# A macaron transformer on one core: products of the second attention moved into its bursts, its norm steps moved to GpSimd

## The chip, the cores and the metric

The kernel runs on one core of one Trainium2 chip. The metric is the device time of one launch in microseconds. The core has TensorE (PE, matmuls and transposes, results to PSUM), VectorE (DVE), ScalarE (ACT), GpSimd (POOL) and SyncE (SP). Each engine takes its instructions in the order of its own queue, and engines are tied by semaphores only.

## The reference, cut to what matters

The input is 8 x 512 tokens of 128 numbers. Six blocks follow one another, each on the normalized x and each added to x:

```
x = x + 0.5 * ffn0(norm(x));  x = x + attn0(norm(x));  x = x + 0.5 * ffn0(norm(x))
x = x + 0.5 * ffn1(norm(x));  x = x + attn1(norm(x));  x = x + 0.5 * ffn1(norm(x))
```

The change is in attn1, the second attention. It has 16 heads of 8 numbers and compares every query of a sequence with every key by a hyperbolic distance:

```
diff_sq  = max(q_norm_sq + k_norm_sq - 2.0 * qk, 0.0)
denom    = max((1.0 - q_norm_sq) * (1.0 - k_norm_sq), 1e-06)
cosh_arg = max(1.0 + 2.0 * diff_sq / denom, 1.0)
attn     = softmax(-arccosh(cosh_arg)); out = (attn @ v) @ Wo.T
```

After it comes the layer norm of the new x (mean and variance over the 128 numbers), and router logits for the last block.

## The kernel before, in words

x stays in SBUF for the whole launch (X, tokens on partitions; XT, the normalized x turned round). The phases F0a, A0, F0b, F1a, A1, F1b follow one another, with a barrier between them. A1 (`attn1`, from line 1106) is the phase of the change. One iteration of its loop is one chunk: 512 tokens, one sequence. `main(0, True)` is the first chunk, without a predecessor; a loop runs `main(c, False)` for chunks 1 to 7, and code behind the loop finishes chunk 7.

For each head a 512x512 square of scores is made in two halves, so a chunk has 32 halves, numbered n. PE makes the squared distance (`difference(n)`, 28 rows of KT and QT, line 1592) and the factor 1/denom (`factor(n)`, 9 rows, line 1604). DVE takes the first with a clamp (`relu`, line 1455) into a U slot and multiplies the second in (`scale`, line 1463). ACT makes from a whole head two square roots (lines 1418 and 1419), POOL adds their results (`add`, line 1373), and ACT takes a logarithm and an exponential (lines 1428 and 1430), into a Y slot. PE multiplies Y with the values (`outputs`, line 1576), where the two heads of a pair use different columns; pair p is heads 2p and 2p + 1. There are four U slots (relu of head h waits for the add of head h - 4) and six Y slots (the first root of head h waits for the products of the pair that used the slot).

The order of the work is written by hand, engine by engine. DVE and PE go in four bursts a chunk, each for four heads, eight halves, steps i = 0 to 7. In step i PE issues `difference(n0 + i + 1)` (i from 1 to 6), `factor(n0 + i)` and then whatever `after(i)` holds; DVE does the next relu, the scale, and its own `after(i)`. The stretches between bursts are called gaps here:

- Burst 0 holds turns (transposes of the assembled q and k rows, line 1307, copied by DVE at line 1315) in steps 0 to 3. In the gap behind it the next chunk's q, k and values are projected (line 1200) and taken by DVE (`take_q_vector`, `take_k_vector`, `take_v_vector`, lines 1224 to 1252), with products of pairs 6 and 7 of the chunk before between the projections.
- Burst 1 holds the turning and dividing of the chunk before's output. In the gap behind it come the output projection, the addition to x (line 465), the norm's statistics (lines 115 to 120, ending in var_eps) and products of pairs 0 and 1.
- Burst 2 holds the norm: `norm_apply_vector` (line 126) in step 1, the turn of the normed rows in step 3, the router logits in step 5. POOL makes rstd (line 140) between the adds of heads 3 and 4.
- The gap behind burst 2 has four turns with products of pairs 2 and 3 between them, burst 3 four more turns, and the gap behind it four turns with products of pairs 4 and 5 of the chunk before (the calls stand at the top of the next `main`).

ACT works in groups of four heads: eight roots, a table load, four pairs of logarithm and exponential, a table load. At the start of A1 POOL copies the first rows of x, clears the row buffers QA and KA (lines 1359 and 1360, memory of the last phase's weights) and VA, and writes constant columns; DVE waits for all of it (`pad_ready`) before its first take. Of a row of 64 numbers in QA and KA the matmuls use numbers 0 to 27 and 32 to 40 only.

Of the kernel before, what the change touches and what calls it, by code (L numbers as in the profile page):

```python
# [5 lines left out]
ALU = mybir.AluOpType  # L6
# [7 lines left out]
P = 128  # L14
# [20 lines left out]
def macaron(nc, x, alpha, w_qkv0, bias_rows0, wo0, wo0_t, wfc0, router0, expert_bias, up0, down0,  # L35
            w_qkv1, wo1, router1, up1, down1, out, stop_after=99):
    ctx = ExitStack()
    with ctx:
# [1090 lines left out]
        def attn1():  # L1129
# [14 lines left out]
            with ExitStack() as st:  # L1144
# [172 lines left out]
                def early_bank(i):  # L1317
                    return (i + 2) % 6

                (turn_out_tensor, divide_vector, turn_back_tensor, _, project_out_tensor,  # L1320
                 residual_vector) = tail_steps(s, lay, lambda t, g: OT[:, g, t * P:(t + 1) * P], on, oT, rden[:, :], ROWS)
# [5 lines left out]
                def turn_norm_tensor(eng, n):  # L1327
                    eng.wait_ge(s["xn_ready"], n + 1)
                    eng.wait_ge(s["x_added"], n)
                    for t in range(TPC):  # L1330
                        last = eng.transpose(ps[:, ROWS, t * P:(t + 1) * P], xn[:, t, :], ident[:, :])
                    last.then_inc(s["tr_done"], 1)

# [21 lines left out]
                def body(block):  # L1355
                    @block.gpsimd
                    def _(eng):
                        eng.tensor_copy(xa[:, :], XT[:, 0:S]).then_inc(s["xa_ready"], 1)
                        eng.memset(QA.rearrange("p h r -> p (h r)").bitcast(F32), 0.0)
                        eng.memset(KA.rearrange("p h r -> p (h r)").bitcast(F32), 0.0)  # L1360
                        eng.memset(VA[:, :], 0.0)
                        eng.drain()
                        eng.memset(QA[:, :, 26:28].bitcast(F32), 1.0)
                        eng.memset(KA[:, :, 24:26].bitcast(F32), 1.0)
                        eng.memset(KA[:, :, 40:41].bitcast(F32), FAR)
                        eng.memset(VA[:, 0:TPC * H * VC].rearrange("p (h r) -> p h r", r=VC)[:, :, HD:HD + 1], 1.0)
# [9 lines left out]
                        def main(c, first):  # L1376
# [5 lines left out]
                            if not first:  # L1382
                                norm_gpsimd(eng, s, c)
# [15 lines left out]
                        norm_gpsimd(eng, s, B)  # L1399
# [39 lines left out]
                    def _(eng):  # L1439
# [6 lines left out]
                        def main(c, first):  # L1446
# [64 lines left out]
                            if tail:  # L1511
                                residual_vector(eng, c, before_c)
                                norm_stats_vector(eng, s, c, before_c)
# [21 lines left out]
                        eng.wait_ge(pad_ready, 1)  # L1535
# [13 lines left out]
                        residual_vector(eng, B, B - 1)  # L1549
                        norm_stats_vector(eng, s, B, B - 1)  # L1550
                        norm_apply_vector(eng, s, B, B - 1)
# [5 lines left out]
                    def _(eng):  # L1557
# [23 lines left out]
                        def main(c, first):  # L1581
# [68 lines left out]
                            if not first:  # L1650
                                outputs(c - 1, 6, (0, 1))
                            eng.wait_ge(s["q_taken"], c + 2)
                            project_rows_tensor(eng, xa, 1, ROWS, "k_done")
                            if not first:
                                outputs(c - 1, 6, (2, 3))
                                outputs(c - 1, 7, (0, 1, 2, 3))
# [4 lines left out]
                            def after1(i):  # L1661
                                if first:
# [48 lines left out]
                        project_rows_tensor(eng, xa, 1, 7, "k_done")  # L1711
                        eng.wait_ge(s["asm_done"], 1)
# [8 lines left out]
                        for pair in range(4, PAIRS):  # L1721
# [79 lines left out]
```

## Time and profile before

| | us |
|---|---|
| three runs, median (lowest, highest) | 3533.08 (3528.67, 3537.28) |
| the profiled execution: time | 3532.39 |
| the profiled execution: span | 3530.7 |
| busy: PE | 2876.4 |
| busy: DVE | 2279.0 |
| busy: ACT | 1908.5 |
| busy: POOL | 850.3 |
| mean granted clock of TensorE, share of full | 0.837 |
| phase A1, first and last activation of ACT in it | 1848.0 and 3065.2 (starts) |

Times in the rows are microseconds from the start of the span. Busy time of PE counts overlapping matmul records once, and a busy PE need not be at its peak. The granted clock is given as a share of 2.4 GHz: 0.50 is 1.2 GHz. In brackets behind a row stands how long the engine had been idle before it, and which instruction ended that.

### The profile page before, as it was taken

The page shows a single profiled execution, that of the slowest core. Times are in us where ns is not written, and L with a number is a line of the kernel's source. Part 1 is how long each engine was busy: PE and PEld are TensorE (multiplying, and loading weights), DVE is VectorE, ACT ScalarE, POOL GpSimd, SP SyncE. Part 2 cuts the span into 40 slices and gives each one's busy share as a digit, 9 for nine tenths or more (in the row PEclk, how much of TensorE's full clock was granted, in tenths as well). Part 3 has the DMA queues.
Part 4 walks back from the last instruction along what each step waited for, and adds up shares of the span by engine and source line. Part 5 has one row for each costly group of instructions (what it writes and reads, how often), then busy time and mean ns, then how long its engine had stood idle before and what let it go on. Part 6 is the DMA issues. An engine that isn't in the chain of part 4 may idle for free. (4 is left out here: it accounts for less than half of the span.)

```text
span 3530.7 us, 52885 instructions
## 1 busy us (share of the span) xinstructions
PE 2876.4 (81%) x17862; PEld 2183.2 (62%) x17862; DVE 2279.0 (65%) x5078; ACT 1908.5 (54%) x2244; POOL 850.3 (24%) x546
## 2 busy tenths in 40 slices
PE   5999968888599996999966767767676776679999
PEld 4888856666488885999952333333333333269998
DVE  5555557777555556666656776776676777366665
ACT  2222257676422222334318888887888888633333
POOL 1000010000000001000025555554655555410000
PEclk9999979999799997999975666666666666689999
DMA  2000000000000001000000000000000000010000
GB/s 78 0 0 0 0 1 1 0 0 0 0 1 0 0 0 48 0 0 0 0 0 0 1 1 0 0 0 0 0 0 0 0 0 0 0 48 0 0 0 24
DMA packets 3189, 17.98 MB, mean 5 GB/s; under 512 B 1088, under 2 KB 2112, under 8 KB 2112
## 3 DMA queue, kind: packets, MB, share of 16 engines
q1 hardware_dynamic: 3136, 17.32, 1.3%
q8 instruction: 28, 0.46, 0.1%
q14 instruction: 25, 0.20, 0.0%
HBM read 15.22 MB, written 2.10 MB: 5 GB/s over the span
## 5 line engine op out<-in xcount | busy, mean ns | idle before, releaser
L1373 POOL TENSOR_TENSOR A_Y<-A_Y,A_U 128x2048 f32<-128x2048 f32 x96 | 433.5, 4541 | 419.5 <-ACT A_U L1419 419.5
L1604 PE MATMUL ps<-A_QT,A_KT 9*128 9x512 f32 x512 | 294.3, 671 | 247.4 <-DVE A_U L1463 247.4
L1455 DVE TENSOR_SCALAR A_U<-ps 128x1024 f32<-128x1024 f32 x256 | 309.0, 1217 | 81.2 <-POOL A_Y L1373 50.4
L140 POOL TENSOR_TENSOR rstd<-var_eps,half_neg 128x4 f32<-128x4 f32 x45 | 49.8, 1107 | 1277.9 <-DVE var_eps L120 1277.9
L1604 PEld LDWEIGHTS ps<-A_QT,A_KT 9*128 9x128 f32 x512 | 120.0, 290 | 376.8 <-DVE A_U L1463 354.7
L1463 DVE SCALAR_TENSOR_TENSOR A_U<-ps,A_U 128x1024 f32<-128x1024 f32 x256 | 311.7, 1218 | 49.3 <-PE ps L1604 49.3
L1592 PE MATMUL ps<-A_QT,A_KT 28*128 28x512 f32 x512 | 269.7, 662 | 88.2 <-DVE A_U L1455 86.8
L257 ACT ACTIVATE F1b_act<-ps 128x512 f32<-128x512 f32 x256 | 153.3, 599 | 247.4 <-PE ps L223 231.4
L257 ACT ACTIVATE F1a_act<-ps 128x512 f32<-128x512 f32 x256 | 153.3, 599 | 242.9 <-PE ps L223 226.6
L257 ACT ACTIVATE F0b_act<-ps 128x512 f32<-128x512 f32 x160 | 95.7, 598 | 273.1 <-PE ps L223 273.1
L1419 ACT ACTIVATE A_U<-A_U 128x2048 f32<-128x2048 f32 x128 | 242.5, 1894 | 0.0
L231 PEld LDWEIGHTS ps<-dn,F1a_hT 128*128 128x128 f32 x2048 | 237.2, 192 | 4.4
L231 PEld LDWEIGHTS ps<-dn,F1b_hT 128*128 128x128 f32 x2048 | 237.2, 192 | 4.4
L257 ACT ACTIVATE F0a_act<-ps 128x512 f32<-128x512 f32 x160 | 95.7, 598 | 266.1 <-PE ps L223 266.1
L231 PE MATMUL ps<-dn,F1a_hT 128*128 128x128 f32 x2048 | 237.6, 275 | 0.0
L231 PE MATMUL ps<-dn,F1b_hT 128*128 128x128 f32 x2048 | 237.6, 275 | 0.0
L1418 ACT ACTIVATE A_Y<-A_U 128x2048 f32<-128x2048 f32 x96 | 182.5, 1901 | 80.7 <-DVE A_U L1463 51.4
L841 ACT ACTIVATE A_M<-A_M,A_nmax 128x192 f32<-128x192 f32 (+1 forms) x512 | 203.9, 471 | 35.4 <-DVE A_nmax L956 34.1
L1592 PEld LDWEIGHTS ps<-A_QT,A_KT 28*128 28x128 f32 x512 | 126.1, 294 | 133.2 <-DVE A_U L1455 107.2
L956 DVE CUSTOM_DVE_ANT_0 A_M<-ps,A_mask 128x192 f32<-128x192 f32 (+1 forms) x512 | 169.2, 387 | 48.0 <-PE ps L1007 47.2
L1576 PE MATMUL ps<-A_Y,A_VA 128*32 128x512 f32 x768 | 176.2, 672 | 17.1 <-ACT A_Y L1430 17.1
L1430 ACT ACTIVATE A_Y<-A_Y 128x2048 f32<-128x2048 f32 x96 | 183.4, 1911 | 6.5
(334 smaller groups left out, 6673.0 us busy)
## 6 DMA issues: line engine op xcount, KB each, us to landing
dn<-in_down SPq DMA_DIRECT2D x2, 2048.0 KB, 12.0
stage<-in_up SPq DMA_DIRECT2D x1, 2560.0 KB, 9.2
X<-in_x SPq DMA_DIRECT2D x1, 2048.0 KB, 7.8
F1a_up<-in_up SPq DMA_DIRECT2D x1, 2048.0 KB, 7.8
F1b_up<-in_up SPq DMA_DIRECT2D x1, 2048.0 KB, 7.3
out_x<-X SPq DMA_DIRECT2D x1, 2048.0 KB, 6.3
dn<-in_down SPq DMA_DIRECT2D x1, 1280.0 KB, 11.9
qkv_w_s<-in_w_qkv SPq DMA_DIRECT2D x2, 192.0 KB
```

The source lines that it names most:

```text
L231: last = eng.matmul(ps[:, 4 + d % 2, t * P:(t + 1) * P], hT[:, d % 2, hb, t * P:(t + 1) * P], dn[:, d, hb, :], start=(hb == 0), stop=(hb = ...
L257: eng.activation(act_out[:, j % RING, :], ps[:, (j * G) % 4, :], ACT.Silu if lay == 0 else ACT.Relu).then_inc(s["act_done"], 1)
L841: last = eng.activation(m, m, ACT.Exp, scale=-1.0, bias=nmax[:, n % MR, b, r:r + 1])
L1373: eng.tensor_tensor(flat(y_slot(h)), flat(y_slot(h)), flat(Um[:, h % UR]), ALU.add).then_inc(s["t_ready"], 1)
L1418: eng.activation(y, u, ACT.Sqrt, bias=1.0)
L1419: eng.activation(u, u, ACT.Sqrt).then_inc(s["s_ready"], 1)
L1430: eng.activation(y, y, ACT.Exp, scale=-1.0 if square_on_vector(h) else -2.0).then_inc(s["y_exp"], 1)
L1455: eng.tensor_scalar(u_half(h, half), d_pair(n), 0.0, None, ALU.max).then_inc(s["dp_vector"], 1)
L1463: eng.scalar_tensor_tensor(out=u, in0=g_pair(), scalar=CLAMP, in1=u, op0=ALU.min, op1=ALU.mult).then_inc(s["u_ready"], 1)
L1576: last = eng.matmul(ps[j:j + 32, OUT, :], VA[:, v0:v0 + 32], y_slot(h)[:, kt, :], start=(kt == 0), stop=(kt == TPC - 1))
L1592: last = eng.matmul(ps[:, 2 * (n % 2) + b, :], KT[r:r + 28, h // 2, kt * P:(kt + 1) * P], QT[r:r + 28, h // 2, :], start=True, stop=True)
L1604: last = eng.matmul(ps[:, 4 + b, :], KT[r:r + 9, h // 2, kt * P:(kt + 1) * P], QT[r:r + 9, h // 2, :], start=True, stop=True)
```

## The change

- The two halves of the products of pairs 0, 2, 4 and 6 (the first pair of each group of four heads) leave the gaps. They are issued behind `factor` in steps 5 and 6 of a burst: pair 6 of the chunk before in burst 0, pair 0 in burst 1, pair 2 in burst 2, pair 4 in burst 3. The products of pair 7 are spread over the two places where pair 6 was.
- The addition of the attention's output goes to xa (a buffer of q's input, free by then) and not into X (`add_back_vector`), and the statistics are taken from xa. POOL makes rstd, then subtracts and multiplies in four instructions, and copies xa into X (`apply_norm_gpsimd`). DVE no longer does these steps in burst 2.
- The clearings of QA and KA are left out, the constant columns are written first, and the wait for `pad_ready` moves from DVE to PE, behind the first projections.

```diff
+                def add_back_vector(eng, n, chunk):
+                    eng.wait_ge(s["o_done"], n)
+                    eng.tensor_tensor(xa[:, :].rearrange("p (t d) -> p t d", d=D), tiles_of(chunk),
+                                      ps[:, ROWS, :].rearrange("p (t d) -> p t d", d=D), ALU.add).then_inc(s["x_added"], 1)
+                    eng.drain()
+                    for t in range(TPC):
+                        eng.bn_stats(bn[:, t, :], xa[:, t * D:(t + 1) * D])
+                    eng.drain()
...
+                def apply_norm_gpsimd(eng, n, chunk):
+                    norm_gpsimd(eng, s, n)
+                    eng.drain()
+                    for t in range(TPC):
+                        eng.tensor_scalar(xn[:, t, :], xa[:, t * D:(t + 1) * D], mv[:, t, 0:1], rstd[:, t:t + 1],
+                                          ALU.subtract, ALU.mult)
+                    eng.drain().then_inc(s["xn_ready"], 1)
+                    eng.tensor_copy(tiles_of(chunk), xa[:, :].rearrange("p (t d) -> p t d", d=D))
+                    eng.drain()
...
-                        eng.memset(QA.rearrange("p h r -> p (h r)").bitcast(F32), 0.0)
-                        eng.memset(KA.rearrange("p h r -> p (h r)").bitcast(F32), 0.0)
-                        eng.memset(VA[:, :], 0.0)
-                        eng.drain()
                         eng.memset(QA[:, :, 26:28].bitcast(F32), 1.0)
                         eng.memset(KA[:, :, 24:26].bitcast(F32), 1.0)
                         eng.memset(KA[:, :, 40:41].bitcast(F32), FAR)
+                        eng.memset(VA[:, :], 0.0)
+                        eng.drain()
...
                             if not first:
-                                norm_gpsimd(eng, s, c)
+                                apply_norm_gpsimd(eng, c, last_chunk(c))
...
                             def after2(i):
-                                if tail and i == 1:
-                                    norm_apply_vector(eng, s, c, before_c)
...
-                        eng.wait_ge(pad_ready, 1)
                         take_q_vector(eng, 0, 6)
...
                             turn(c, EARLY)
-                            if not first:
-                                outputs(c - 1, 4, (0, 1))
                             turn(c, EARLY + 1)
-                            if not first:
-                                outputs(c - 1, 4, (2, 3))
...
                             def after0(i):
                                 if i < 4:
                                     turn(c, EARLY + 4 + i)
+                                if not first and i in (5, 6):
+                                    outputs(c - 1, 6, (2 * i - 10, 2 * i - 9))
...
                             def after1(i):
+                                if i in (5, 6):
+                                    outputs(c, 0, (2 * i - 10, 2 * i - 9))
...
-                            outputs(c, 0, (0, 1, 2, 3))
                             outputs(c, 1, (0, 1, 2, 3))
 
                             def after2(i):
+                                if i in (5, 6):
+                                    outputs(c, 2, (2 * i - 10, 2 * i - 9))
...
                             turn(c + 1, 0)
-                            outputs(c, 2, (0, 1))
                             turn(c + 1, 1)
-                            outputs(c, 2, (2, 3))
...
                             def after3(i):
                                 if i < 4:
                                     turn(c + 1, 4 + i)
+                                if i in (5, 6):
+                                    outputs(c, 4, (2 * i - 10, 2 * i - 9))
...
                         project_rows_tensor(eng, xa, 1, 7, "k_done")
+                        eng.wait_ge(pad_ready, 1)
                         eng.wait_ge(s["asm_done"], 1)
```

## Rows read from the trace of the kernel before

**Rows 1.** Windows, one chunk of A1: stretch, length, busy by engine, clock, DMA.

```profile
2006.27:2159.89 153.62, 109.28 (x386) 52.57 (x384) 109.08 (x122) 128.35 (x72) 83.58 (x45) 0.64 0.00 0
```

**Rows 2.** Timeline of ACT: start, length, instruction, idle time before it.

```profile
2006.27 1.28 ACT L1418 ACT_TABLE_LOAD   x1 [12.57 <-PE ps L1576]
...
2088.40 1.91 ACT L1418 ACTIVATE dn<-A_U 128x2048 f32<-128x2048 f32 x1 [8.80 <-PE ps L1576]
...
2123.70 1.91 ACT L1418 ACTIVATE A_Y<-A_U 128x2048 f32<-128x2048 f32 x1 [2.82 <-PE ps L1576]
...
2138.08 1.91 ACT L1430 ACTIVATE A_Y<-A_Y 128x2048 f32<-128x2048 f32 x1
...
2159.89 1.28 ACT L1418 ACT_TABLE_LOAD   x1 [12.34 <-PE ps L1576]
```

**Rows 3.** Timeline of DVE over the same chunk and the next burst 0.

```profile
2015.99 2.35 DVE L1455 TENSOR_SCALAR A_U<-ps 128x1024 f32<-128x1024 f32 x2 [6.19 <-POOL A_Y L1373]
...
2043.73 0.17 DVE L120 TENSOR_SCALAR var_eps<-mv 128x4 f32<-128x4 f32 x1
...
2049.68 2.36 DVE L1455 TENSOR_SCALAR A_U<-ps 128x1024 f32<-128x1024 f32 x2 [1.87 <-POOL dn L1373]
...
2056.44 7.25 DVE L126 TENSOR_SCALAR xn<-X,mv,rstd 128x128 f32 x4
...
2079.74 1.23 DVE L1463 SCALAR_TENSOR_TENSOR A_U<-ps,A_U 128x1024 f32<-128x1024 f32 x1 [1.31 <-PE ps L1604]
...
2093.78 2.35 DVE L1455 TENSOR_SCALAR A_U<-ps 128x1024 f32<-128x1024 f32 x2
...
2115.36 1.22 DVE L1463 SCALAR_TENSOR_TENSOR A_U<-ps,A_U 128x1024 f32<-128x1024 f32 x1 [1.31 <-PE ps L1604]
...
2129.08 2.34 DVE L1455 TENSOR_SCALAR A_U<-ps 128x1024 f32<-128x1024 f32 x2
...
2150.51 1.22 DVE L1463 SCALAR_TENSOR_TENSOR A_U<-ps,A_U 128x1024 f32<-128x1024 f32 x1 [1.31 <-PE ps L1604]
```

**Rows 4.** Timeline of PE: a projection, products at either clock, factors of burst 0.

```profile
1997.79 2.08 PE L1200 MATMUL ps<-qkv_w_s,A_xa 128*128 128x128 f32 x8
...
2081.60 3.63 PE L1576 MATMUL ps<-dn,A_VA 128*32 128x512 f32 x8
...
2088.79 1.91 PE L1576 MATMUL ps<-A_Y,A_VA 128*32 128x512 f32 x8
...
2144.19 0.79 PE L1604 MATMUL ps<-A_QT,A_KT 9*128 9x512 f32 x1 [1.57 <-DVE A_U L1463]
...
2149.25 0.79 PE L1604 MATMUL ps<-A_QT,A_KT 9*128 9x512 f32 x1 [1.32 <-DVE A_U L1463]
```

**Rows 5.** Windows of 2 us; the eighth number is the granted clock.

```profile
2084.30:2086.30 2.00, 2.00 (x10) 0.81 (x8) 0.00 (x0) 0.00 (x0) 0.79 (x1) 0.50 0.00 0
2086.30:2088.30 2.00, 2.00 (x9) 0.42 (x10) 0.69 (x1) 0.00 (x0) 0.00 (x0) 0.94 0.00 0
...
2104.30:2106.30 2.00, 2.00 (x9) 1.49 (x10) 2.00 (x3) 2.00 (x2) 0.00 (x0) 0.50 0.00 0
```

**Rows 6.** Groups of instructions of POOL by shape: count, busy, mean ns.

```profile
L1288 POOL TENSOR_SCALAR A_sides<-A_nrm 128x128 f32<-128x128 f32 x9 | 5.9, 658 | 0.0
...
L1212 POOL COPY A_xa<-XT 128x512 f32 x7 | 4.3, 611 | 1.9 <-issue 1.9
...
L1263 POOL TENSOR_SCALAR A_nrm<-A_nrm 128x128 f32<-128x128 f32 x9 | 2.7, 301 | 0.0
```

**Rows 7.** Timeline of the start of A1, all engines.

```profile
1801.19 3.52 POOL L1359 MEMSET up_hi<- 128x4096 f32 x1
...
1801.41 3.76 PE L1200 MATMUL ps<-qkv_w_s,A_xa 128*128 128x128 f32 x16 [2.47 <-POOL A_xa L1358]
...
1809.88 1.23 DVE L1224 CAST up_hi<-ps 128x1024 fp32r<-128x1024 f32 x1 [12.11 <-POOLq L1367]
```

**Rows 8.** Timeline of DVE behind the last chunk of A1.

```profile
3084.83 1.11 DVE L126 TENSOR_SCALAR xn<-X,mv,rstd 128x128 f32<-128x128 f32 x4 [1.16 <-POOL rstd L140]
```

More of the change, by code:

```diff
@@ L1318, in early_bank @@
                     return (i + 2) % 6
-                (turn_out_tensor, divide_vector, turn_back_tensor, _, project_out_tensor,
-                 residual_vector) = tail_steps(s, lay, lambda t, g: OT[:, g, t * P:(t + 1) * P], on, oT, rden[:, :], ROWS)
+                (turn_out_tensor, divide_vector, turn_back_tensor, _, project_out_tensor, _) = tail_steps(s, lay, lambda t, g: OT[:, g, t * P:(t + 1) * P], on, oT, rden[:, :], ROWS)
                 def copy_back_vector(eng, n):
@@ L1332, in turn_norm_tensor @@
                     last.then_inc(s["tr_done"], 1)
+                def add_back_vector(eng, n, chunk):
[7 more added lines that the diff above has]
+                    for t in range(TPC):
+                        eng.bn_aggr(mv[:, t, :], bn[:, t, :])
+                    eng.drain()
+                    eng.tensor_scalar(var_eps[:, :], mv[:, :, 1], EPS, None, ALU.add).then_inc(s["var_ready"], 1)
+                def apply_norm_gpsimd(eng, n, chunk):
+                    norm_gpsimd(eng, s, n)
+                    eng.drain()
+                    for t in range(TPC):
+                        eng.tensor_scalar(xn[:, t, :], xa[:, t * D:(t + 1) * D], mv[:, t, 0:1], rstd[:, t:t + 1],
[3 more added lines that the diff above has]
+                    eng.drain()
                 def copy_norm_vector(eng, n):
@@ L1365, in _ @@
                         eng.memset(KA[:, :, 40:41].bitcast(F32), FAR)
+                        eng.memset(VA[:, :], 0.0)
+                        eng.drain()
                         eng.memset(VA[:, 0:TPC * H * VC].rearrange("p (h r) -> p h r", r=VC)[:, :, HD:HD + 1], 1.0)
@@ L1398, in _ @@
                             main(c, False)
-                        norm_gpsimd(eng, s, B)
+                        apply_norm_gpsimd(eng, B, B - 1)
                         keep_norm_gpsimd(eng, B, B - 1)
@@ L1511, in main @@
                             if tail:
-                                residual_vector(eng, c, before_c)
-                                norm_stats_vector(eng, s, c, before_c)
+                                add_back_vector(eng, c, before_c)
                             out_copy_vector(eng, c, 0)
                             def after2(i):
-                                if tail and i == 1:
-                                    norm_apply_vector(eng, s, c, before_c)
                                 if tail and i == 3:
@@ L1548, in _ @@
                         copy_back_vector(eng, B)
-                        residual_vector(eng, B, B - 1)
-                        norm_stats_vector(eng, s, B, B - 1)
-                        norm_apply_vector(eng, s, B, B - 1)
+                        add_back_vector(eng, B, B - 1)
                         copy_norm_vector(eng, B)
@@ L1650, in main @@
                             if not first:
-                                outputs(c - 1, 6, (0, 1))
+                                outputs(c - 1, 7, (0, 1))
                             eng.wait_ge(s["q_taken"], c + 2)
@@ L1654, in main @@
                             if not first:
-                                outputs(c - 1, 6, (2, 3))
-                                outputs(c - 1, 7, (0, 1, 2, 3))
+                                outputs(c - 1, 7, (2, 3))
                             eng.wait_ge(s["k_taken"], c + 2)
@@ L1720, in _ @@
                             main(c, False)
-                        for pair in range(4, PAIRS):
+                        for pair in range(5, PAIRS):
                             outputs(B - 1, pair, (0, 1, 2, 3))
```

## The prediction

> **What bounds the kernel now.** I read the windows first. The changed attention runs about 154 us per chunk, seven such periods after a first chunk; in one, ScalarE is busy 128.4 us, TensorE and VectorE 109 each, GpSimd 84 [rows 1]. The nearest limit is thus ScalarE, with 25 us to lose per period. Its timeline shows where they sit: 12.34 us ahead of the table load that opens a chunk, 8.80 ahead of head 10, 2.82 ahead of head 14, each ended by attention products on PE, which free a Y slot [rows 2]. But ScalarE's waits are a symptom. Following the releases back (VectorE's timeline, then PE's) gives a loop that closes in exactly 153.6 us through VectorE and PE [rows 3]:
> burst 0 start to burst 1 start 40.5 (2129.08 to 2015.99 + 153.6: burst 22.6, the q, k, v copies 11.8, then 6.2 of waiting for GpSimd's first add); burst 1 start to var_eps 27.9; var_eps to burst 2 start 5.8 (rstd, first add); burst 2 31.2 (to 2080.9); gap 12.9; burst 3 22.7 (to 2116.5); gap 12.6.
> In the bursts VectorE is full until the last two steps; in the gaps it idles while PE turns rows and multiplies. So what counts per period is how much PE work is hidden beside VectorE.
>
> The clock matters as much. A half of a pair's products (8 records) takes 3.63 us at granted clock 0.5 and 1.91 at 1.0 [rows 4]. The windows show clock 0.50 at 2104.3 with PE busy 2.00 of 2.00 us on the score matmuls, and a rise to 1.0 at about 2086.5, some 6 us after turns and products began [rows 5].
>
> **Products moved into the bursts (steps 5 and 6).** No work is added: 64 of 128 product records per period move. In burst 0 of before, factor 5 starts at 2144.19 and occupies PE 1.2 us; VectorE then has one scale (1.13) left until it needs difference 7, now queued behind the first half. Cold, step by step: half 2145.3 to 2148.9; difference 7 beside factor 6 to 2150.1; relu 7 and scale 6 to 2152.6; second half beside them to 2153.6; factor 7 to 2154.8; scale 7 ends 2156.0, where it ended 2151.6 [rows 3, 4]. So 7.1 us of products cost 4.4: only 2.7 are hidden. With both halves at clock 1.0 the burst grows 0.7; with only the second at 1.0, 2.5.
> What leaves the gaps: with bursts 2 and 3 followed by three turns (each waits for its copy, about 0.85 us exposed, which products hid before) and one product pair, a gap is 13.5 us cold, 8.0 warm (turns and copies to the third turn, then the 5.6 us that the row 2088.79 begins), against 12.9 and 12.6. After bursts 0 and 1 nothing is won: there the moved products lay beside VectorE's copies, or beside GpSimd's add.
> Which clock? A half of 3.6 us is shorter than the rise took, half plus half plus the scores between is longer. I take: first half and most of the second cold, clock up when the burst ends, so +4.4 per burst and 8.0 per gap; the ends are kept for the range.
>
> **Burst 0 to 1.** ScalarE's head 0 now waits for pair 6 inside burst 0: ready 24.7 us after its start, head 0 at 26, first add done at 34.3; VectorE is ready at 22.6 + 4.4 + 11.8 - 0.8 (q projection at the higher clock, from 2.08 us [rows 4]) = 38.0. The 6.2 wait is gone; 40.5 becomes 38.0. Burst 1 loses 1.0 of waits for adds, gains 4.9 (turn back sits behind the second half), and 1.3 off for turn back and output projection at clock 1.0: 27.9 becomes 30.5.
> The products' new wait is for both exps of the pair. Head 13's ends at 2140.0, pair 6 would be issued at 2145.3 [rows 2, 4]; the other pairs have more room. Behind it on PE stand factors 6 and 7, so a miss would stop VectorE; I cost it at nothing.
>
> **Norm on GpSimd.** Four 128x128 subtract-multiplies with per-partition scalars and a 128x512 copy stand before the add of head 4. No row has such an instruction; the nearest are 0.30 (contiguous) and 0.66 us, the copy is 0.61 [rows 6]. I take 0.45 each, 1.8, plus 0.61 and three drains of 0.13: +2.8 (ends +2.2 and +3.7): 5.8 becomes 8.6. VectorE loses the same four from burst 2: they take 7.25 us at 2056.44 [rows 3] and 1.11 when GpSimd is idle [rows 8]. They end as GpSimd's adds end. The Trainium skill (GPSIMD Engine Reference, Key points) says GpSimd shares SBUF interfaces with VectorE instructions in a 2-port mode; the trace agrees (7.25 against 1.11), and by it the removal is worth more than the 1.1 of work. Burst 2 without them, but paced by adds 4.55 apart, is 24.0; with products and score in one queue 28.0. The later adds make ScalarE wait about 5 us in heads 4 to 7; it still has room, as the loop leaves it 18 us idle.
> The same skill (same page, Engine selection) says elementwise belongs on VectorE, GpSimd being about twice as slow with two inputs. These are one-input steps, so it moves the sum only within the ends above.
>
> **Period:** 38.0 + 30.5 + 8.6 + 28.0 + 8.0 + 27.1 + 8.0 = 148.2 against 153.6: -5.4.
>
> **Once only.** The two clearings (3.52 us each) go, and VectorE no longer waits for them: q is projected by about 1803.5, the first copy starts at 1809.88 [rows 7]: -6.3, all on the path, because ScalarE has nothing before. The wait on the pads moves to PE, ahead of a later wait: nothing. First chunk: three bursts +4.4, three gaps -3.7, -4.9, -4.6: 0. Head 0 of chunk 1 comes 26 us after its burst start, before 32.1: -6.1. Six periods -32.4. Last chunk: ScalarE idle 9.6 becomes 7.3: -2.3. Tail: norm on GpSimd where VectorE took 1.11 with nothing beside [rows 8]: +0.9.
> Sum: -6.3 - 6.1 - 32.4 - 2.3 + 0.9 = -46.2. The profiled run took 3532.4 (span 3530.7), the median of the shown runs is 3533.1, so both give 3486.
>
> **Rivals.**
> *Clock up early (0.2).* The first half brings PE to 1.0: bursts +2.5, gaps 8. Period 36.1 + 28.1 + 8.6 + 25.2 + 8.0 + 25.2 + 8.0 = 139.2, six times -14.4; first chunk -5.7, the rest -13.8: 3427. For it: at clock 1.0 PE has slack in every burst. Against: the rise of [rows 5] came some 6 us after its run began. If it were at 1.0 throughout, ScalarE's own 130 (busy and table steps) plus 5 of waits would bound a period at about 135, six times -18.6: near 3390. The Trainium skill (TensorE: Matmul & The Clock Gate, Part 1) has a busy engine released to 2.4 GHz; by that alone this would be the likeliest case, but 2104.3 shows a fully busy PE at 0.50, so it gets 0.2.
> *Clock low (0.17), slower than before.* The products are cut into pieces with score matmuls between, so the long runs that raised the clock in the gaps are gone; it rises only near the gap's end. Bursts +4.4 and a gap 12.5: period 38.8 + 31.8 + 8.6 + 28.0 + 12.5 + 27.1 + 12.5 = 159.3, six times +5.7; first chunk +9.9 (three bursts +13.2, gaps -3.3), the rest -12.5: +31.6, 3564. It decides from gaps of more than 9.7 us, where the period equals the old one. Cold to the end of the gaps: +46, 3578.
> *GpSimd price (0.1).* The pointer-scalar instructions cost about 1.1 us like the 128x4 pow; the norm ends 2.6 later, eight times: 3507.
> *Hidden anyway (0.1).* Lengthened bursts return exactly what gaps give; prologue alone stays: 3526.
> *Forecast (0.43).* 3486.
>
> This kernel's measurement tells 0.2%, 7 us, from nothing. Faster: 0.2 + 0.43 + 0.1 and a third of the hidden case, 0.76; same 0.07; slower 0.17. The range 3425 to 3545 reaches the early clock, the GpSimd price and part of the slow case; the forecast's own is 3465 to 3510.
>
> **What would show it.** Products issued in step 5, first half about 3.6 us, second mixed; bursts of 27 us, gaps of 8; period 148; VectorE's wait before burst 1 gone; ScalarE's wait ahead of the chunk's first table load still there (near 11 us) and that of head 10 gone; GpSimd's four steps near 0.45; granted clock up in the gaps. Wrong if the clock in the bursts is 1.0 or stays 0.5 through the gaps, if PE waits for exps in step 5, or if ScalarE never idles.

## The result, and the profile after

| | before | changed |
|---|---|---|
| median of 14 runs each, us | 3532.6 | 3524.1 |
| lowest to highest | 3528.6 to 3538.1 | 3515.7 to 3527.9 |
| profiled execution, span | 3530.7 | 3514.0 |
| one period of the loop | 153.6 | 153.6 |

The ratio is 0.9972 with a 95% interval from 0.9963 to 0.9981: 8.5 us faster, where 46 were forecast. The sign was right, the size was not. Of the 16.7 us between the two spans 5.9 lie ahead of the changed phase (its first table load stands at 1794.77, before at 1800.62), in code that is the same (in e_clear's profiled execution it stands at 1805.62), so about 11 are the change's in this execution.

They were won once and not per chunk. From the phase's first table load to its first root the changed kernel is 6.5 us faster, to the table load that opens chunk 1 another 9.0; the six periods behind that take what they took, and the last chunk and the tail lose 4.2. The windows of the changed kernel show the second, the third and the sixth of these periods:

```profile
2138.40:2292.00 153.60, 120.14 (x386) 49.88 (x388) 101.58 (x117) 128.80 (x73) 87.26 (x50) 0.64 0.00 0
2292.00:2445.60 153.60, 120.12 (x386) 49.87 (x388) 101.57 (x117) 128.80 (x73) 87.30 (x50) 0.64 0.00 0
2752.80:2906.40 153.60, 120.12 (x386) 49.86 (x388) 101.58 (x117) 128.81 (x73) 87.26 (x50) 0.64 0.00 0
```

Against [rows 1] VectorE has 7.5 us less work, GpSimd 3.7 more, PE shows 11 us more busy time for the same number of matmuls (386), and the period is the same.

VectorE's timeline of the changed kernel gives the segments. L1475 is the relu, L1483 the scale; the rows answer to [rows 3]. The end of a burst is taken as in the prediction, 0.1 us ahead of the end of its last row.

```profile
2113.68 2.35 DVE L1475 TENSOR_SCALAR A_U<-ps 128x1024 f32<-128x1024 f32 x2
...
2134.75 1.22 DVE L1475 TENSOR_SCALAR A_U<-ps 128x1024 f32<-128x1024 f32 x1 [3.48 <-PE ps L1606]
...
2139.20 1.23 DVE L1483 SCALAR_TENSOR_TENSOR A_U<-ps,A_U 128x1024 f32<-128x1024 f32 x1 [2.10 <-PE ps L1618]
...
2150.57 2.35 DVE L1475 TENSOR_SCALAR A_U<-ps 128x1024 f32<-128x1024 f32 x2
...
2177.05 1.23 DVE L1483 SCALAR_TENSOR_TENSOR A_U<-ps,A_U 128x1024 f32<-128x1024 f32 x1
...
2181.18 0.17 DVE L1344 TENSOR_SCALAR var_eps<-mv 128x4 f32<-128x4 f32 x1
...
2191.59 2.36 DVE L1475 TENSOR_SCALAR A_U<-ps 128x1024 f32<-128x1024 f32 x2 [8.70 <-POOL dn L1393]
...
2213.62 0.19 DVE L135 TENSOR_TENSOR logits<-ps,ebias 128x32 f32 x1 [4.25 <-PE ps L1368]
...
2218.47 1.23 DVE L1483 SCALAR_TENSOR_TENSOR A_U<-ps,A_U 128x1024 f32<-128x1024 f32 x1 [1.45 <-PE ps L1618]
...
2230.16 2.35 DVE L1475 TENSOR_SCALAR A_U<-ps 128x1024 f32<-128x1024 f32 x2
...
2255.48 1.23 DVE L1483 SCALAR_TENSOR_TENSOR A_U<-ps,A_U 128x1024 f32<-128x1024 f32 x1 [1.89 <-PE ps L1618]
```

| segment, us | before | forecast | changed |
|---|---|---|---|
| burst 0 start to burst 1 start | 40.5 | 38.0 | 36.9 |
| burst 1 start to var_eps | 27.9 | 30.5 | 30.8 |
| var_eps to burst 2 start | 5.8 | 8.6 | 10.2 |
| burst 2 | 31.2 | 28.0 | 28.0 |
| gap | 12.9 | 8.0 | 10.6 |
| burst 3 | 22.7 | 27.1 | 26.4 |
| gap | 12.6 | 8.0 | 10.7 |
| period | 153.6 | 148.2 | 153.6 |

The 3.48 and 2.10 us ahead of the last relu and scale of burst 0 are VectorE waiting for a difference and a factor that stand behind the products on PE.

PE's timeline of the changed kernel, in the gap behind burst 3 (L1307 turns, L1590 products):

```profile
2102.23 0.66 PE L1307 MATMUL ps<-ident,up_hi 128*128 128x128 f32 x4
2103.77 0.66 PE L1307 MATMUL ps<-ident,up_lo 128*128 128x128 f32 x4 [0.87 <-DVE A_QT L1315]
2105.21 1.11 PE L1307 MATMUL ps<-ident,up_hi 128*128 128x128 f32 x4 [0.78 <-DVE A_KT L1315]
2106.25 3.63 PE L1590 MATMUL ps<-dn,A_VA 128*32 128x512 f32 x8
2109.81 1.12 PE L1307 MATMUL ps<-ident,up_lo 128*128 128x128 f32 x4
2110.86 2.17 PE L1590 MATMUL ps<-dn,A_VA 128*32 128x512 f32 x8
```

and the windows of the same stretch, where the eighth number is the granted clock:

```profile
2102.00:2104.00 2.00, 1.13 (x8) 0.66 (x7) 1.71 (x2) 2.00 (x2) 0.29 (x1) 1.00 0.00 0
2104.00:2106.00 2.00, 1.22 (x8) 0.89 (x6) 0.69 (x1) 2.00 (x2) 0.91 (x1) 0.65 0.00 0
2106.00:2108.00 2.00, 2.00 (x8) 0.41 (x8) 0.69 (x1) 2.00 (x2) 2.00 (x1) 0.50 0.00 0
2110.00:2112.00 2.00, 2.00 (x9) 0.83 (x10) 0.69 (x1) 1.93 (x2) 2.00 (x1) 0.65 0.00 0
```

The clock did come up as the burst ended, as forecast, and the first turn takes 0.66 us. But PE then waits twice for a copy (0.87 and 0.78), the clock is back at 0.50 by the third turn (1.11), and the products there run cold, that is at 0.50: 3.63 us for the first half. Before, products stood between these turns, PE had no such waits, and once the clock was up it stayed up to the end of the gap (1.00 in each window of 2 us from 2122 to 2130):

```profile
2117.83 3.31 PE L1576 MATMUL ps<-A_Y,A_VA 128*32 128x512 f32 x8
2121.07 0.66 PE L1307 MATMUL ps<-ident,up_lo 128*128 128x128 f32 x4
2121.66 1.91 PE L1576 MATMUL ps<-A_Y,A_VA 128*32 128x512 f32 x8
```

GpSimd and ScalarE around the norm:

```profile
2181.43 1.05 POOL L140 TENSOR_TENSOR rstd<-var_eps,half_neg 128x4 f32<-128x4 f32 x1 [14.96 <-DVE var_eps L1344]
2182.68 3.14 POOL L1350 TENSOR_SCALAR xn<-A_xa,mv,rstd 128x128 f32<-128x128 f32 x4 [0.20 <-issue]
2186.14 0.61 POOL L1353 COPY X<-A_xa 128x512 f32 x1 [0.33 <-issue]
2186.97 9.00 POOL L1393 TENSOR_TENSOR dn<-dn,A_U 128x2048 f32<-128x2048 f32 x2 [0.22 <-ACT A_U L1439]
```

```profile
2101.30 1.91 ACT L1438 ACTIVATE A_Y<-A_U 128x2048 f32<-128x2048 f32 x1 [4.50 <-PE ps L1590]
...
2138.40 1.28 ACT L1438 ACT_TABLE_LOAD   x1 [13.24 <-PE ps L1590]
...
2191.49 1.91 ACT L1448 ACTIVATE dn<-dn 128x2048 f32<-128x2048 f32 x1 [3.39 <-POOL dn L1393]
```

One of the four steps costs 0.79 us and not 0.45. ScalarE's wait of 8.80 ahead of head 10 [rows 2] is 0.39 now; the others are there still (13.24 ahead of the chunk, 4.50 ahead of head 14), and 3.39 for the late add is new.

### The profile page after: what moved, and what is told of

Same layout as the page of the kernel before. It is cut to its first block and busy times, and to the rows that moved or that the text cites. A ratio compares the mean times of both kernels' runs of the same rounds, so it can differ in the third digit from the quotient of the medians.

```text
span 3514.0 us, 52886 instructions
## 1 busy us (share of the span) xinstructions
PE 2944.6 (84%) x17862; PEld 2157.0 (61%) x17862; DVE 2225.0 (63%) x5046; ACT 1911.2 (54%) x2244; POOL 872.9 (25%) x584
## 5 line engine op out<-in xcount | busy, mean ns | idle before, releaser
L1475 DVE TENSOR_SCALAR A_U<-ps 128x1024 f32<-128x1024 f32 x256 | 309.3, 1219 | 161.4 <-PE ps L1606 92.7
L1618 PE MATMUL ps<-A_QT,A_KT 9*128 9x512 f32 x512 | 274.7, 629 | 123.4 <-DVE A_U L1483 123.4
L1483 DVE SCALAR_TENSOR_TENSOR A_U<-ps,A_U 128x1024 f32<-128x1024 f32 x256 | 311.9, 1218 | 51.4 <-PE ps L1618 51.4
L1606 PE MATMUL ps<-A_QT,A_KT 28*128 28x512 f32 x512 | 250.4, 612 | 95.3 <-DVE A_U L1475 93.8
L1590 PE MATMUL ps<-A_Y,A_VA 128*32 128x512 f32 x768 | 271.8, 851 | 14.2 <-ACT A_Y L1450 14.2
L1618 PEld LDWEIGHTS ps<-A_QT,A_KT 9*128 9x128 f32 x512 | 112.7, 272 | 257.2 <-DVE A_U L1483 210.1
L1606 PEld LDWEIGHTS ps<-A_QT,A_KT 28*128 28x128 f32 x512 | 112.6, 268 | 177.4 <-DVE A_U L1475 116.5
```

The costliest lines, as they stand in the source:

```text
L1475: eng.tensor_scalar(u_half(h, half), d_pair(n), 0.0, None, ALU.max).then_inc(s["dp_vector"], 1)
L1483: eng.scalar_tensor_tensor(out=u, in0=g_pair(), scalar=CLAMP, in1=u, op0=ALU.min, op1=ALU.mult).then_inc(s["u_ready"], 1)
L1590: last = eng.matmul(ps[j:j + 32, OUT, :], VA[:, v0:v0 + 32], y_slot(h)[:, kt, :], start=(kt == 0), stop=(kt == TPC - 1))
L1606: last = eng.matmul(ps[:, 2 * (n % 2) + b, :], KT[r:r + 28, h // 2, kt * P:(kt + 1) * P], QT[r:r + 28, h // 2, :], start=True, stop=True)
L1618: last = eng.matmul(ps[:, 4 + b, :], KT[r:r + 9, h // 2, kt * P:(kt + 1) * P], QT[r:r + 9, h // 2, :], start=True, stop=True)
```

## The experiments

Each was timed against the kernel before on its chip; a period is from one burst 0 to the next, the steady ones of one profiled execution. Diffs are against the changed kernel unless said otherwise.

| kernel | median | ratio, 95% interval | period |
|---|---|---|---|
| e_clear | 3526.6 | 0.9979 [0.9968, 0.9990] | 153.6 |
| e_norm | 3510.5 | 0.9942 [0.9925, 0.9959] | 150.2 |
| e_products | 3513.1 | 0.9940 [0.9922, 0.9959] | 150.2 |
| e_undo_norm | 3499.9 | 0.9911 [0.9892, 0.9930] | 150.2 |
| e_less | 3480.1 | 0.9841 [0.9822, 0.9859] | 146.8 |
| e_more | 3511.8 | 0.9936 [0.9919, 0.9953] | 151.9 |
| e_order | 3475.9 | 0.9832 [0.9815, 0.9848] | 146.8 |
| e_fill | 3464.2 | 0.9799 [0.9770, 0.9827] | 143.4 to 146.8 |
| e_gapprod | 3477.2 | 0.9848 [0.9831, 0.9864] | 146.8 |
| e_one | 3483.2 | 0.9849 [0.9833, 0.9866] | 146.5 to 147.2 |
| e_late | 3486.3 | 0.9851 [0.9830, 0.9873] | 146.8 to 149.5 |
| e_order_dve | 3473.8 | 0.9831 [0.9815, 0.9847] | 146.8 |
| e_order_gap6 | 3501.1 | 0.9908 [0.9892, 0.9925] | 146.4 to 156.4 |
| e_order1 | 3455.3 | 0.9774 [0.9757, 0.9791] | 143.35 |
| e_best | 3455.4 | 0.9779 [0.9763, 0.9795] | 143.35 |

**The parts alone.** e_clear: the clearings and the pad wait, all else as before.

```diff
-                        eng.memset(QA.rearrange("p h r -> p (h r)").bitcast(F32), 0.0)
-                        eng.memset(KA.rearrange("p h r -> p (h r)").bitcast(F32), 0.0)
...
-                        eng.wait_ge(pad_ready, 1)
                         take_q_vector(eng, 0, 6)
```

> Only the two clearings and the moved wait, all else as before. My theory (the prologue is on the path, all of it): 6.5 us faster than before, 3526, as the first root of ScalarE came 6.5 earlier behind the phase's start in the changed kernel; the period stays at 153.6. Rival (the start of the first burst shifts against the clock's rises, and a later gap gives the gain back): within 3 us of before.

Measured: 4.7 us by the medians, 3.5 to 11.3 by the interval; the theory's 6.5 lies in it, the period is unchanged. What is won once at the start stays won.

e_norm: before, with `apply_norm_gpsimd` and `add_back_vector` alone, and without `norm_apply_vector` in burst 2.

```diff
-                                norm_gpsimd(eng, s, c)
+                                apply_norm_gpsimd(eng, c, last_chunk(c))
...
-                                residual_vector(eng, c, before_c)
-                                norm_stats_vector(eng, s, c, before_c)
+                                add_back_vector(eng, c, before_c)
```

> Only the norm is moved to GpSimd; products in the gaps and clearings as before. Theory: var_eps to burst 2 grows from 5.8 to 10.2, burst 2 shrinks from 31.2 to 24.0, so the period is 150.8 and six of them win 17: 3516. Rival (the GpSimd price eats what VectorE wins): period 153 to 154, 3533.

Measured: 21 us, period 150.2. The gap behind burst 1 and burst 2 together went from 41.3 to 38.9 (14.6 and 24.3, before 10.1 and 31.2), a gain of 2.4; the gaps behind bursts 2 and 3 gave another 0.9. The theory held to 0.6 us of period.

e_products: before, with only the products moved.

```diff
+                                if i in (5, 6):
+                                    outputs(c, 0, (2 * i - 10, 2 * i - 9))
...
-                            outputs(c, 0, (0, 1, 2, 3))
```

(and so for pairs 2, 4 and 6).

> Only the products are moved; norm on VectorE and clearings as before. Theory (segments of the changed trace add up: 36.9 + 30.8 + 5.8 + about 35 with the norm steps of 7.2 back in burst 2 + 10.6 + 26.5 + 10.7): period 156.3, slower than before by 16 in six periods, less some 9 won once in the first chunk: 3540. Rival (the moved products are a gain that the norm on GpSimd eats): period below 152, under 3520.

Measured: 18 us faster, period 150.2 from chunk 3 on, where the sum gave 156.3 and a loss. This miss is the key to the case. In the period of chunk 1 (153.7) burst 0 is 26.6 and burst 3 26.3 long with gaps of 10.5 and 10.6, as in the changed kernel; the period of chunk 2 is 151.8; from chunk 3 on burst 0 is 25.0, burst 3 25.3 and the last gap 9.7. The same instructions, in the same order, take 3.5 us less.

Three parts, 5, 21 and 18 us alone, make 8.5 together.

**Why the parts do not add.** e_undo_norm: the changed kernel with the norm steps back on VectorE.

```diff
                             if tail:
-                                add_back_vector(eng, c, before_c)
+                                residual_vector(eng, c, before_c)
+                                norm_stats_vector(eng, s, c, before_c)
...
-                                apply_norm_gpsimd(eng, c, last_chunk(c))
+                                norm_gpsimd(eng, s, c)
```

> The changed kernel with its norm steps back on VectorE; products in the bursts and clearings left out. Theory (the norm move wins nothing where products set burst 2, and in the changed kernel it shifts PE against the clock's rises so that bursts 0 and 3 and a gap run colder): period 150.2 as with the products alone, 3505, faster than the changed kernel. Rival (the norm move is worth its 2.4 us here too and something else in the combination is slow): period 156, 3540.

Measured: 3499.9, period 150.2 from chunk 3 on. The theory's time was met to 5 us: beside the moved products the norm's move costs 22 (by the ratios) to 24 us (by the medians), while alone it won 21. On its own segments it wins 0.4 there: the gap behind burst 1 and burst 2 are 8.9 + 32.9 with it on VectorE and 13.4 + 28.0 on GpSimd. The theory's reason, that the products alone set the length of burst 2, is not what the rows show. With the norm on VectorE its four steps still take 7.3 us there, and PE waits 8.2 us for them; the first half of the products starts 23.4 us into the burst, and 16.4 with the norm on GpSimd. So the move wins its 7 us in this place too, and 4.5 go to the longer gap ahead of it. The rest is lost behind it: from the first half to the end of the burst it is 9.5 us with the norm on VectorE and 11.6 on GpSimd, because the clock is up earlier in the first case (L1368 is the router's matmul, L1595 the products):

```profile
2363.88 3.50 PE L1595 MATMUL ps<-dn,A_VA 128*32 128x512 f32 x8
2367.31 1.06 PE L1368 MATMUL ps<-rw,xT_c 128*128 128x8 f32 x8
...
2368.96 1.91 PE L1595 MATMUL ps<-dn,A_VA 128*32 128x512 f32 x8
```

In the changed kernel the same three take 3.63, 1.88 and 3.21 (their rows are below). The 3.8 us per period that the move costs elsewhere are colder matmuls too: burst 0 (26.6 against 25.0, second half 3.63 against 1.91), burst 3 (26.4 against 25.3, the same halves) and the last gap (10.7 against 9.7).

e_less takes the copy of xa into X off the path; e_more makes it three times.

```diff
                     eng.drain().then_inc(s["xn_ready"], 1)
+
+                def keep_sum_gpsimd(eng, chunk):
                     eng.tensor_copy(tiles_of(chunk), xa[:, :].rearrange("p (t d) -> p t d", d=D))
                     eng.drain()
...
                             assemble_gpsimd(eng, c + 1)
+                            if not first:
+                                keep_sum_gpsimd(eng, last_chunk(c))
```

> The changed kernel with the copy of xa into X (0.61 us and a drain, 0.85 on the path ahead of the add of head 4) moved behind the adds of heads 4 to 7. Plain sum: period 152.75, 5 us faster than the changed kernel, 3519. Theory (the period is tied to where the clock rises): not 152.75, but 153.6 again, or 150.2 with 3503, if the shift lets a rise come one burst step earlier.

```diff
-                    eng.tensor_copy(tiles_of(chunk), xa[:, :].rearrange("p (t d) -> p t d", d=D))
-                    eng.drain()
+                    for _ in range(3):
+                        eng.tensor_copy(tiles_of(chunk), xa[:, :].rearrange("p (t d) -> p t d", d=D))
+                        eng.drain()
```

> The changed kernel with that copy made three times in place (1.7 us more on the path). Plain sum: period 155.3, 10 us slower than the changed kernel, 3534. Theory (tied to the clock's rises): not 155.3; 153.6 again if the added time is absorbed by a shorter cold stretch, else about 157 and 3544.

Measured: less work gave 3480.1 and a period of 146.8, more work gave 3511.8 and 151.9. Both are faster than the changed kernel. The plain sum (152.75 and 155.3) fails in both, and so did the guess of where they would settle (150.2 or 153.6; 153.6 or 157). In e_more the path from var_eps to burst 2 grew by 1.5 as built, and burst 2 and, by turns, burst 0 or the last gap became shorter by about 1.6 each. In e_less the path lost 0.9 between var_eps and burst 2 as built; the other 5.9 are burst 0 (26.7 to 25.0), burst 2 (28.0 to 25.9), burst 3 (26.4 to 25.3) and the last gap (10.7 to 9.7). Its PE timeline in burst 2 (L1595 products, L1370 the router's matmul) shows how:

```profile
2357.92 3.43 PE L1595 MATMUL ps<-dn,A_VA 128*32 128x512 f32 x8
2361.29 1.06 PE L1370 MATMUL ps<-rw,xT_c 128*128 128x8 f32 x8
...
2362.94 1.91 PE L1595 MATMUL ps<-dn,A_VA 128*32 128x512 f32 x8
```

against the changed kernel's:

```profile
2208.04 3.63 PE L1590 MATMUL ps<-dn,A_VA 128*32 128x512 f32 x8
2211.60 1.88 PE L1368 MATMUL ps<-rw,xT_c 128*128 128x8 f32 x8
...
2214.56 3.21 PE L1590 MATMUL ps<-dn,A_VA 128*32 128x512 f32 x8
```

In e_less the clock comes up at the end of the first half, and the router's matmul and the second half run in 1.06 and 1.91; in the changed kernel it comes up only within the second half, and they take 1.88 and 3.21. VectorE stands behind all of it.

**Is it the gap's clock?** e_order keeps everything and lets products stand between the first turns.

```diff
                             turn(c + 1, 0)
+                            outputs(c, 3, (0, 1))
                             turn(c + 1, 1)
+                            outputs(c, 3, (2, 3))
                             turn(c + 1, 2)
-                            outputs(c, 3, (0, 1))
                             turn(c + 1, 3)
-                            outputs(c, 3, (2, 3))
```

(and the same for pair 5 at the top of `main`).

> The changed kernel with the products of pairs 3 and 5 moved within the gap: turn, products, turn, products, turn, turn instead of three turns first. Theory (the granted clock falls to 0.50 in the gap because PE only waits for copies there, and the products run half of it cold; with products between the first turns the copies are hidden and the clock stays up): gaps 8 to 9 instead of 10.6, period 149 to 151, 3500 to 3510. Rival (clock falls anyway): gaps 10.6, period 153.6, 3524.

Measured: 3475.9, gaps 7.4 and 8.0, period 146.8: more than the theory asked. The windows of its gap show the clock up to the end, and all turns and products run warm:

```profile
2070.00:2072.00 2.00, 2.00 (x14) 0.74 (x12) 0.69 (x1) 2.00 (x2) 2.00 (x1) 1.00 0.00 0
2074.00:2076.00 2.00, 1.54 (x8) 0.93 (x9) 1.25 (x3) 1.97 (x3) 2.00 (x1) 1.00 0.00 0
```

```profile
2068.63 1.91 PE L1590 MATMUL ps<-A_Y,A_VA 128*32 128x512 f32 x8
2070.47 0.66 PE L1307 MATMUL ps<-ident,up_lo 128*128 128x128 f32 x4
2071.06 1.91 PE L1590 MATMUL ps<-A_Y,A_VA 128*32 128x512 f32 x8
2072.90 0.66 PE L1307 MATMUL ps<-ident,up_hi 128*128 128x128 f32 x4
2074.34 0.66 PE L1307 MATMUL ps<-ident,up_lo 128*128 128x128 f32 x4 [0.79 <-DVE A_QT L1315]
```

This is the forecast's gap of 8.0, which the changed kernel's order did not have. The gaps give 5.8 of the 6.8 us, burst 3 the other 1.0 (its second half takes 1.91).

e_order also hides two copies, so it alone does not part the clock from the waits. e_fill does: it leaves the order, and adds work.

```diff
-                            ahead(3)
+                            difference(24)
...
                             turn(c + 1, 0)
+                            fill(c * HALVES + 24)
                             turn(c + 1, 1)
+                            fill(0)
                             turn(c + 1, 2)
+                            difference(25)
```

`fill` is four transposes of the identity into a free bank; the gap behind burst 3 (at the top of `main`) has two as well.

> The changed kernel with four extra transposes of the identity into a free bank behind the first and the second turn of the gaps after bursts 2 and 3, and the second difference after the third turn. They compute nothing that is used. Theory (clock): with PE kept at full-array work the clock stays at 1.0 and the gaps, at worst longer by 0.3 us of filler each, fall from 10.6 to about 8.5; period 149 to 151. Rival (extra work only lengthens the queue, the clock is not kept by it): gaps 11, period 154 to 157, over 3524.

Measured: 3464.2, gaps 8.4, periods 143.4 and 146.8 in turn. Sixteen more transposes a chunk whose results nobody reads make the changed kernel 60 us faster. Its PE timeline in the gap (L1644 is the filler):

```profile
2101.15 0.66 PE L1307 MATMUL ps<-ident,up_hi 128*128 128x128 f32 x4
2101.64 0.60 PE L1644 MATMUL ps<-ident 128*128 128x128 f32 x4
2102.59 0.66 PE L1307 MATMUL ps<-ident,up_lo 128*128 128x128 f32 x4 [0.35 <-DVE A_QT L1315]
2103.08 0.60 PE L1644 MATMUL ps<-ident 128*128 128x128 f32 x4
2104.03 0.66 PE L1307 MATMUL ps<-ident,up_hi 128*128 128x128 f32 x4 [0.35 <-DVE A_KT L1315]
...
2105.28 1.91 PE L1590 MATMUL ps<-dn,A_VA 128*32 128x512 f32 x8
```

The windows of the same stretch, with the clock at 1.00 throughout:

```profile
2102.00:2104.00 2.00, 1.34 (x11) 0.86 (x9) 1.23 (x2) 2.00 (x2) 2.00 (x1) 1.00 0.00 0
2104.00:2106.00 2.00, 1.97 (x10) 0.97 (x12) 0.69 (x1) 2.00 (x2) 2.00 (x2) 1.00 0.00 0
```

The turns start 1.44 us apart, in the changed kernel 1.54 and 1.44 (2102.23, 2103.77, 2105.21): the filler takes next to nothing off the copies' latency. What is shorter is the third turn (0.66, was 1.11) and the products' first half (1.91, was 3.63). The filler needs a free bank, so a score difference of the gap also moved behind the third turn; that it would not shorten these by itself was not tried apart. With this one reserve the cost of the gap was the clock. The two gaps give 4.4 us of period; the rest of the win lies in the bursts, where the clock is then up earlier (burst 0 is 25.3, in some chunks burst 1 24.6 and burst 3 25.0).

**Which products belong into a burst.** e_gapprod puts pairs 2 and 4 back into the gaps; e_one puts pair 0 back too.

```diff
                             def after2(i):
...
-                                if i in (5, 6):
-                                    outputs(c, 2, (2 * i - 10, 2 * i - 9))
...
                             turn(c + 1, 0)
+                            outputs(c, 2, (0, 1))
                             turn(c + 1, 1)
+                            outputs(c, 2, (2, 3))
                             turn(c + 1, 2)
```

> The changed kernel with pairs 2 and 4 back in the gaps as before; pairs 6 and 0 stay in bursts 0 and 1. Theory (in bursts 2 and 3 the products cost VectorE 4 us each and give back only 2 in the gap): 36.9 + 30.8 + 10.2 + 24.0 + 12.9 + 22.7 + 12.6 = 150.1, six times -3.5, with the prologue and first chunk about 3500. Rival (in the bursts they are hidden as well as in the gaps, the period is set elsewhere): 153.6 and 3524 like the changed kernel.

> The changed kernel with only pair 6 left inside a burst (burst 0); pairs 0, 2 and 4 in the gaps as before. Theory (pair 0 is hidden beside GpSimd's norm and add in the gap after burst 1 and costs burst 1 about 1 to 3 us): burst 1 22.5, its gap 13.5 to 14.6; period 144 to 146, 3460 to 3475. Rival (pair 0 in the gap delays the copy of the output bank behind it, or the clock then rises later): period 147 to 150, 3477 or more.

Measured: 3477.2 (period 146.8, sum 150.1) and 3483.2 (146.5 to 147.2, sum 144 to 146). In e_gapprod the gaps are 12.4 and 12.2 and bursts 2 and 3 24.3 and 22.7, near the sum's 12.9, 12.6, 24.0 and 22.7; burst 1 is 24.7 where the changed kernel has 27.6, with the same products in it, because the clock comes up earlier there (halves of 3.24 and 1.91 against two of 3.63). In e_one burst 1 is 23.0 (the theory had 22.5), but the gap behind it grows by 1.2, and in one period of three the gap behind burst 0 by 1.7, so nothing is won, as its rival said. e_late is e_gapprod with the copy off the path as in e_less:

> As the kernel with pairs 6 and 0 in the bursts (period 146.8), and the copy of xa back into X (0.61 us and a drain) moved behind the adds of heads 4 to 7. Theory of the plain sum: the path from var_eps to burst 2 is 0.8 shorter, so the period is 146.0, 5 us in six periods. Rival (the period is tied to where the clock rises, small savings are given back as a longer cold stretch): 146.8 again, under 2 us.

Here the same 0.9 us won nothing: the ratio is that of e_gapprod within the intervals (0.9851 and 0.9848), and in the profiled execution the periods go from 146.8 to 149.5 and six of them take 6.6 us more than e_gapprod's. Both theories missed, and with e_less this shows that the worth of such a saving isn't to be had from the path. One of its four launches took 9011 us; what held it up is not known, the interval leaves it out, and the median of the other three is 3485.1.

**The better versions.** e_order1 is e_order with pair 0 in the gap behind burst 1, e_best has one `fill` behind the third turn of the gaps behind bursts 2 and 3 besides, e_order_dve is e_order with the norm on VectorE, e_order_gap6 is e_order with pairs 6 and 0 in the gaps.

```diff
                             def after1(i):
-                                if i in (5, 6):
-                                    outputs(c, 0, (2 * i - 10, 2 * i - 9))
...
                                 project_out_tensor(eng, c)
+                            outputs(c, 0, (0, 1, 2, 3))
                             outputs(c, 1, (0, 1, 2, 3))
```

> The kernel with the reordered gaps (period 146.8) with pair 0 back in the gap after burst 1. Theory (there it lies beside GpSimd's norm and add): burst 1 27.6 to 23.0, its gap 13.4 to 14.6, period 143.4, 20 us faster than with pair 0 in the burst: 3455. Rival (as with pair 6 alone in a burst, the clock then rises later and burst 0 or a gap takes it back): period 146 to 147, 3470 or more.

> Reordered gaps, pair 0 in the gap, and four unused transposes behind the third turn of the gaps after bursts 2 and 3, to keep PE at full-array work. Theory (clock): the gaps stay at 7.4 to 8 with the clock up, period 143.4 or less, 3440 to 3455. Rival (the filler only adds 0.6 us to each gap): period 144.5, 3460 or more.

> The kernel with the reordered gaps and the norm steps back on VectorE. Theory (with products in burst 2 PE, not VectorE, sets its length, so the move to GpSimd wins there only what it costs ahead of it: 13.4 + 28.0 against 8.9 + 32.9): period 147.2, within 5 us of 3476. Rival (the move wins its 2.4 us of period also here, as it did alone): period 149 to 150, 3490 or more.

> The kernel with the reordered gaps, and pairs 6 and 0 back in the gaps after bursts 0 and 1; only pairs 2 and 4 in bursts. Theory (without pair 6 in burst 0 the first root of ScalarE comes late and VectorE waits 6 us again for GpSimd's first add): burst 0 22.7 and 18.0 behind it, against 26.7 and 10.2: 3.8 longer there, 3.4 shorter around burst 1: period 147 to 147.5, 3478. Rival (pair 6 in burst 0 is worth nothing, as it costs what it saves): period 143.4 as with pair 0 in the gap alone.

Measured: e_order1 3455.3, period 143.35, as its theory had it: 77 us under the kernel before. e_best is the same within the interval, and so is its period of 143.35: the two gaps are 7.0 each and 1.5 us shorter together, and burst 3 is 1.2 longer (its second half takes 3.63 and not 1.91), bursts 0 and 2 0.3 together. What the gaps gain is given back at the clock. e_order_dve 3473.8 against e_order's 3475.9: here the norm's place makes no difference, and its own segments are as above (8.9 + 32.9 and 13.4 + 28.0). e_order_gap6 3501.1: without pair 6 in burst 0 the 18 us behind burst 0 are back (ScalarE's first root waits for it, VectorE 6.19 for the add), and no two periods in a row are alike (146.4 to 156.4); its theory's 147 was met to 0.6 in three of six.

## Why the prediction was right or wrong, point by point

- **The loop and its segments** were read rightly: VectorE and PE close the period, ScalarE's waits are a symptom (the 8.8 is gone, nothing was won by that). Burst 2 came out at 28.0 to the tenth, bursts 0 and 3 at 26.6 and 26.4 against 27.0 and 27.1, the cold halves of 3.6 us in step 5 as drawn. A burst with its second half at 1.0 was priced at +2.5, and e_less has 25.0 for burst 0 where 22.6 stood before.
- **The 6.2 us wait behind burst 0** went, as forecast; e_order_gap6 against e_order1 shows that pair 6 in the burst is what removes it.
- **The gap was the step that failed.** "Clock up when the burst ends, so +4.4 per burst and 8.0 per gap" had the rise right and its stay wrong. It had counted the waits for the copies (0.85 us each, measured 0.87 and 0.78), but not what they do to the clock: it fell behind them, and third turn and products ran at 0.50. The gaps are 10.6 and 10.7 instead of 8.0. That is 5.3 us, where the whole forecast was a period shorter by 5.4; the misses of the other segments (-1.1, +0.3, +1.6, 0.0, -0.7) cancel, by luck. e_fill shows the clock as the cause, e_order gives the 8.0. The rival's 12.5 for a low clock was too long: the truth lay between.
- **The norm on GpSimd**: 0.79 us a step where 0.45 was taken from rows of 0.30 and 0.66, so 10.2 instead of 8.6. The rows had no instruction with per-partition scalars; the upper end (+3.7) was not wide enough, +4.4 was measured. The rival of 1.1 us a step was as far off on the other side. The 7.25 us of burst 2 did go (6.9 in e_norm), but e_undo_norm has gap and burst at 8.9 + 32.9 with the norm on VectorE, against 13.4 + 28.0 with it on GpSimd: the products behind the norm ran 2.1 us colder once it was gone, so beside them the move as such won 0.4 us per period.
- **Adding up.** The sum treated the clock as a property of each piece. The period is tied to it: less path time (e_less, -0.9) took 6.8 off the period, more (e_more, +1.5) took 1.7 off. By these two a forecast of this loop by a sum could be right to some 7 us of period only, 40 in the total (an estimate); the range said so, the 3486 did not.
- **Once only**: the prologue gave 6.5 (6.3 forecast). The first chunk and its first head gave 9.0 (6.1), the last chunk and the tail lost 4.2 where 1.4 less was forecast; in the tail ScalarE's idle time grew from 30.4 to 33.6, since nothing hides GpSimd's norm there.
- The rival "hidden anyway" (3526: bursts return what the gaps give, the prologue stays) comes nearest to the measured 3524, with a chance of 0.1. As a balance it holds: bursts +8.7, gaps -8.7. But it gave no reason why they should be equal, so its number is luck: with the gaps of 8.0 that e_order has, the period would not have been the old one.

What stays open: why a given kernel settles at its period. The runs show that it moves with where the clock rises and falls; they do not give a rule by which e_less would be told from e_late in advance, nor say why the changed kernel's period is that of the kernel before.

## What to carry to other kernels

When work moves between stretches of a queue, look at the stretch that it leaves: products between dependent turns hid the copies' latency and kept the clock up, and taking them out cost more than their place in the burst won (e_gapprod, which has those of pairs 2 and 4 back, needs 146.8 a period against 153.6). In a loop whose clock changes within every period, a part measured alone says little of its worth in a combination, so try the order of the work (and a few unused matmuls where PE would only wait) before counting tenths on the path. Of a part that is moved off one engine, ask too at which clock the work behind it will then run.

## What the runs showed of the hardware

- A busy PE is not always at the high clock. In the kernel before PE was busy 8.00 of 8.00 us from 2098 to 2106, with score matmuls of 9 and 28 rows and turns between them, at 0.50. In the gap behind that burst it had turns and products only from 2116.78 on, and the clock was 0.83 in the window from 2120 and 1.00 from 2122. In the changed kernel PE was busy 20.00 of 20.00 us from 2156 to 2176 at 0.50, although two halves of products (2166.97 and 2171.7, 3.63 us each) lie in it.
- It can fall again soon: in the changed kernel it was 1.00 from 2102 to 2104, PE waited 0.87 and 0.78 us for two copies, and it was 0.50 from 2106 to 2108. In e_fill, where the two waits are 0.35 each, it stayed at 1.00.
- The steady periods of these kernels gather at few values: 153.6 (before, changed, e_clear), 150.2 (e_norm, e_products, e_undo_norm), 146.8 (e_order, e_gapprod, e_less, e_order_dve), 143.35 (e_order1, e_best), and are then alike to 0.1 us. e_fill changes between two of these values; in e_more, e_one, e_late and e_order_gap6 the segments change from one period to the next.
- A GpSimd subtract-multiply of 128x128 with per-partition scalars takes 0.79 us, its other one-input steps of that shape, with immediates, 0.30 to 0.66 [rows 6], VectorE's subtract-multiply 0.28 (a quarter of 1.11 in [rows 8]).
